# Low-part loads of a mixture-of-experts stage asked for one run of groups earlier, with two more tables for it

## What is computed

```python
x = x + xattn(layernorm(x), ctx)       # similarities to 1601 context rows, softmax, 2048 -> 512 projection
x = x + attention(layernorm(x))        # 16 heads, causal over 64 tokens
x = x + ffn(layernorm(x))              # below
# ffn: 8 experts, each token goes to its top 2, and a shared expert takes all
logits = x @ w_router.T
expert_weight, expert_idx = top_k(softmax(logits), 2)
inter = square(relu(tokens_of_expert @ w1[e].T))       # 512 -> 512
out_e = inter @ w2[e].T                                # 512 -> 512, times the gate, added to its token
shared = square(relu(x @ ws1.T)) @ ws2.T               # 512 -> 1024 -> 512
```

## Time and profile before

| | |
|---|---|
| median of the runs | 1274.67 us |
| the profiled execution | 1274.44 us, span 1272.7 us |
| TensorE (PE) busy | 1244.0 us, 98% |
| VectorE (DVE) busy | 755.4 us, 59% |
| ScalarE (ACT) busy | 376.5 us, 30% |
| groups of the experts | from 1034 us to 1262 us |
| end | last indirect DMA issued at 1266.45 us |

### The profile page before, as it was taken

One profiled execution on the slowest core, in us unless ns is written; L12 is line 12 of the kernel. 1 busy time (PEld: TensorE's weight loads), 2 busy tenths in 40 slices (PEclk: granted clock), 3 DMA queues, 4 the chain that ended last, 5 costly groups with the idle time before them and its releaser, 6 DMA issues.

```text
span 1272.7 us, 22853 instructions
## 1 busy us (share of the span) xinstructions
PE 1244.0 (98%) x7814; PEld 862.4 (68%) x7815; DVE 755.4 (59%) x1421; ACT 376.5 (30%) x613; POOL 205.1 (16%) x176
## 2 busy tenths in 40 slices
PE   6999999999999999999999999999999999999997
PEld 3444444444444444467888888899989888888886
DVE  3556555655544444478988877857546355555554
ACT  2322211212121111144554554442323233333322
POOL 1000000000000000004222223340531012222222
PEclk9999999999999999999999999999999999999999
DMA  9999999999999999843787788750643678777774
GB/s 357 417 421 419 418 419 422 422 422 421 408 410 389 397 392 393 330 149 107 291 269 261 271 289 313 258 127 1 232 166 132 204 222 186 185 158 158 178 157 92
DMA packets 105433, 358.39 MB, mean 282 GB/s; under 512 B 19872, under 2 KB 40352, under 8 KB 90784
## 3 DMA queue, kind: packets, MB, share of 16 engines
q1 hardware_dynamic: 96880, 337.97, 71.1%
q0 software_dynamic: 8496, 19.73, 7.7%
HBM read 352.80 MB, written 67.78 MB: 330 GB/s over the span
## 4 chain that ended last, share of the span: by engine, by line
PE 83%; DMA 9%; DVE 3%; issue 2%; SPq 1%; ACT 1%; POOL 0%; ACTq 0%; DVEq 0%; POOLq 0%
PE ps L2001 14%; PE ps L1889 13%; PE ps L2073 11%; PE ps L2063 10%; DMA parts_low<-split 5%; PE ps L2363 5%; PE ps L2355 5%; PE ps L2358 5%; PE ps L1964 4%; PE ps L1847 3%; PE ps L1979 2%; DMA high<-parts_low 1%; PE ps L1939 1%; DMA arena<-moe_in 1%; PE ps L1946 1%
## 5 line engine op out<-in xcount | busy, mean ns | idle before, releaser
L2073 PE MATMUL ps<-split 128*128 128x256 f32 x1536 | 194.2, 285 | 3.1 <-DVE split L1336 2.7
L2001 PE MATMUL ps<-arena 128*64 128x512 f32 (+1 forms) x832 | 192.6, 595 | 0.0
L2073 PEld LDWEIGHTS ps<-split 128*128 128x128 f32 x1536 | 187.1, 191 | 8.0 <-issue 6.5
L1889 PE MATMUL ps<-arena 128*64 128x512 f32 (+1 forms) x1024 | 178.7, 505 | 3.9 <-DMA arena<-ctx_t 2.1
L1889 PEld LDWEIGHTS ps<-arena 128*64 128x64 f32 x1024 | 66.0, 138 | 124.2 <-issue 119.4
L2001 PEld LDWEIGHTS ps<-arena 128*64 128x64 f32 (+1 forms) x832 | 58.4, 137 | 112.8 <-issue 112.1
L1232 DVE SCALAR_TENSOR_TENSOR arena<-arena,hbar 128x512 f32<-128x512 f32 x128 | 90.5, 749 | 67.8 <-PE ps L1964 66.1
L768 ACT ACTIVATE arena<-ps 128x512 f32<-128x512 f32 (+1 forms) x93 | 52.3, 581 | 240.5 <-PE ps L1964 180.2
L758 POOL DMA_INDIRECT out<-arena,token_i x39 | 60.5, 1552 | 246.2 <-DVE arena L1803 130.5
L651 POOL TENSOR_TENSOR arena<-arena,row_b 128x512 f32 (+1 forms) x16 | 20.3, 1273 | 476.0 <-DVE arena L1106 448.2
L2063 PE MATMUL ps<-split 128*128 128x512 f32 x384 | 96.9, 401 | 0.1
(11 more groups left out here) (249 smaller groups left out, 1947.3 us busy)
## 6 DMA issues: line engine op xcount, KB each, us to landing
arena<-ctx_t SPq DMA_DIRECT2D x122, 800.5 KB, 14.1
high<-parts_low SPq DMA_DIRECT2D x78, 1024.0 KB
arena<-ctx_n SPq DMA_DIRECT2D x96, 768.0 KB, 10.7
arena<-ctx_n SPq DMA_DIRECT2D x32, 1024.0 KB, 11.6
parts_high<-split SPq DMA_DIRECT2D x16, 1024.0 KB, 8.7
parts_low<-split SPq DMA_DIRECT2D x16, 1024.0 KB, 10.6
moe_in<-zero SPq DMA_DIRECT2D x3, 3328.0 KB, 18.3
stage_raw<-w1t SPq DMA_DIRECT2D x8, 1024.0 KB, 6.5
```

The source lines that it names most:

```text
L1889: last = mm(bank(n)[S * h:S * (h + 1), 0:w], qT[:, k, S * h:S * (h + 1)], ctxT[h][:, k, at_j:at_j + w], start=(k == 0), stop=(k == KD - 1))
L2001: last = mm(bank(7)[S * h:S * (h + 1), :], ET[0:w, c, S * h:S * (h + 1)], ctxN[h][0:w, c, :], start=(c == 0), stop=(c == JC - 1))
L2073: last = mm(dst[:, 2 * P * m:2 * P * (m + 1)], w[a][:, k, c], tokens[b][:, k, :], start=(k + i == 0), stop=(k == KD - 1 and i == 2))
```

## The change

The low parts of the next run are now asked for when a run begins, so that a whole run of groups lies between request and use. For that there are two more tables. `needed_loads`, on DVE behind pair 5 of the shared expert, makes `need_i`: a group's expert with its odd flag, and on top of it the semaphore count at which its low parts are there. TensorE reads this table in place of `eg_i` and waits for that count in a register; it no longer waits for the requests of groups in between. `next_runs`, behind pair 6, makes `next_i`: for each group the expert of the next run, with a flag on the first group of a run, which is where the request moves data. SP reads `next_i` for every request of `w1` and again for every one of `w2`. Both tables lie in memory that is free by then (`causal`, `lg`). There are as many requests and as many moved megabytes as before.

In SP's loop `load_slots(g + 3)` now comes first. Then comes the request for `w1` of group `g + 1`, which brings the next run's part where `g + 1` begins a run, and that for `w2` of group `g`. In iteration 0 the request of group 0 for `w1` stands ahead, behind the slots of group 3. The load of `w2`'s high part of expert 3 goes from before the rows of group 0 to behind them, since the DVE tiles beside which it lies are in use until `next_runs` is done.

```diff
--- before.py
+++ after.py
@@ -107,6 +107,8 @@
 
         slot_i = [sb(f"slot_i{k}", [P, T], I32) for k in range(2)]
         eg_i = sb("eg_i", [P, GT], I32)
+        next_i = lg[:, :, :].rearrange("p t e -> p (t e)")[:, 0:GT].bitcast(I32)
+        need_i = causal[:, 0:GT].bitcast(I32)
         token_i = sb("token_i", [P, GT], I32)
         landed_i = [sb(f"landed_i{i}", [P, GT], I32) for i in range(NY)]
         idx = [[sb(f"idx{k}{i}", [P, 1], I32) for i in range(4)] for k in range(2)]
@@ -544,32 +546,27 @@
             sp.wait_ge(x3_ready, TH)
             store_rows(slice(TH // 2, TH))
 
-            group = {}
-
-            def read_group(g):
-                group[g] = sp.value_load(eg_i[0:1, g:g + 1], min_val=0, max_val=2 * E - 1)
-                group.pop(g - 3, None)
-
-            def load_low(g, parts, places, back):
-
-                odd, e = group[g] >= E, group[g] & (E - 1)
-                if g > 0:
-                    sp.wait_ge(back, 16 * g)
+            def load_low(value, parts, places, back, at, cond):
+
+                odd, e = (value & (2 * E - 1)) >= E, value & (E - 1)
+                if at > 0:
+                    sp.wait_ge(back, 16 * at)
                 sp.dma_start(all_high[:, bass.ds(places[0] + odd * (places[1] - places[0]), KD * D)].bitcast(F32),
-                             parts[bass.ds(e * P, P), :], cond=group[g] != group[g - 1] if g > 0 else None
-                             ).then_inc(back, 16)
-
-            def load_low1(g):
-                load_low(g, parts_low[0], LOW1, low1_back)
-
-            def load_low2(g):
-                load_low(g, parts_low[1], LOW2, low2_back)
-
-            read_group(0)
+                             parts[bass.ds(e * P, P), :], cond=cond).then_inc(back, 16)
+
+            def first_low(parts, places, back):
+                value = sp.value_load(eg_i[0:1, 0:1], min_val=0, max_val=2 * E - 1)
+                load_low(value, parts, places, back, 0, None)
+
+            def next_low(g, parts, places, back):
+                value = sp.value_load(next_i[0:1, g:g + 1], min_val=0, max_val=4 * E - 1)
+                load_low(value, parts, places, back, g + 1, value >= 2 * E)
+
+            first = parts_low[0], LOW1, low1_back
+            second = parts_low[1], LOW2, low2_back
+
             sp.wait_ge(x3_out, 32)
             load_w2(ARENA + KD * D, 7, 8)
-            sp.wait_ge(token_ready, NY)
-            load_w2(3 * KD * D, 3, 4)
             sp.wait_ge(lg_done, T)
             sp.wait_ge(h2lo_ready, T)
             load_w1(1, 2)
@@ -577,7 +574,7 @@
             store_rows(slice(TH, TR))
             for i in range(NH):
                 sp.wait_ge(scat[i], 32 * (T // NH))
-            load_low1(0)
+            first_low(*first)
 
             def load_slots(g):
 
@@ -590,6 +587,8 @@
 
             load_slots(0)
             sp.dma_start(of_slot[:, :, :], info_v).then_inc(info_in, 16)
+            sp.wait_ge(token_ready, 2 + NY)
+            load_w2(3 * KD * D, 3, 4)
             sp.wait_ge(sh_done, 4 * (TA // 2))
             load_w1(0, 1)
             load_w2(0 * KD * D, 0, 2)
@@ -599,26 +598,27 @@
             load_w2(4 * KD * D, 4, 6)
             sp.wait_ge(shlo_ready, 4 * (TA // 2))
             load_slots(2)
-            read_group(1)
             sp.wait_ge(shlo_used, 1)
-            load_low2(0)
+            first_low(*second)
             sp.wait_ge(shared_done, TA)
-            load_low1(1)
             sp.wait_ge(x3_ready, T)
             store_rows(slice(TR, T))
 
             for g in range(GT):
-                if g + 2 < GT:
-                    read_group(g + 2)
-                    sp.wait_ge(in_done, g + 1)
-                    load_low1(g + 2)
                 if g + 3 < GT:
                     sp.wait_ge(xgT_ready, g + 2)
                     load_slots(g + 3)
+                if g == 0:
+                    next_low(0, *first)
+                if g + 2 < GT:
+                    sp.wait_ge(in_done, g + 1)
+                    next_low(g + 1, *first)
                 if g + 1 < GT:
                     if g > 0:
                         sp.wait_ge(y_done, g)
-                    load_low2(g + 1)
+                    next_low(g, *second)
+            sp.wait_ge(low1_back, 16 * GT)
+            sp.wait_ge(low2_back, 16 * GT)
             sp.wait_ge(x3_out, 16 * 4)
 
 
@@ -747,7 +747,7 @@
                             moe_in, bass.IndirectOffsetOnAxis(ap=idx[k][i][:, :], axis=0), hs_rows[i], None
                         ).then_inc(scat[i], 16)
 
-            pool.wait_ge(token_ready, 1 + NY)
+            pool.wait_ge(token_ready, 3 + NY)
             pool.wait_ge(x3_out, 16 * 4)
             for g in range(GT):
                 landed = [pool.value_load(landed_i[i][0:1, g:g + 1], min_val=16, max_val=16 * (GT // NY + 2))
@@ -1745,6 +1745,35 @@
                     step(v.tensor_reduce(landed, passed, AX, ALU.add))
                     v.tensor_scalar(landed_i[i][:, :], landed, 16.0, 16.0, ALU.mult, ALU.add).then_inc(token_ready, 1)
 
+            def needed_loads():
+
+                step(v.tensor_scalar(run, run, NY - 1.0, None, ALU.add))
+                step(v.tensor_tensor(gcmp, run.unsqueeze(2).to_broadcast([P, GT, E]),
+                                     ends.unsqueeze(1).to_broadcast([P, GT, E]), ALU.is_gt))
+                step(v.tensor_tensor(gcmp, gcmp, ends.unsqueeze(1).to_broadcast([P, GT, E]), ALU.mult))
+                step(v.tensor_reduce(rank, gcmp, AX, ALU.max))
+                step(v.tensor_scalar(landed, run, 0.0, None, ALU.is_gt))
+                step(v.tensor_tensor(rank, rank, landed, ALU.add))
+                step(v.scalar_tensor_tensor(eg_f, rank, 2.0 * E, eg_f, ALU.mult, ALU.add))
+                v.tensor_scalar(need_i, eg_f, 2.0 * E, None, ALU.add).then_inc(token_ready, 1)
+
+            def next_runs():
+
+                step(v.tensor_tensor(gcmp, ends.unsqueeze(1).to_broadcast([P, GT, E]),
+                                     iota_g.unsqueeze(2).to_broadcast([P, GT, E]), ALU.is_le))
+                step(v.scalar_tensor_tensor(gcmp, gcmp, 4.0 * GT, ends.unsqueeze(1).to_broadcast([P, GT, E]),
+                                            ALU.mult, ALU.add))
+                step(v.tensor_reduce(rank, gcmp, AX, ALU.min))
+                step(v.tensor_tensor(gcmp, ends.unsqueeze(1).to_broadcast([P, GT, E]),
+                                     rank.unsqueeze(2).to_broadcast([P, GT, E]), ALU.is_le))
+                step(v.tensor_reduce(eg_f, gcmp, AX, ALU.add))
+                step(v.tensor_scalar(eg_f, eg_f, float(E - 1), None, ALU.min))
+                step(v.scalar_tensor_tensor(eg_f, turn, -float(E), eg_f, ALU.mult, ALU.add))
+                step(v.tensor_tensor(landed, run, iota_g, ALU.is_equal))
+                step(v.tensor_scalar(rank, rank, float(GT), None, ALU.is_lt))
+                step(v.tensor_tensor(landed, landed, rank, ALU.mult))
+                step(v.scalar_tensor_tensor(eg_f, landed, 2.0 * E, eg_f, ALU.mult, ALU.add))
+                v.tensor_scalar(next_i, eg_f, float(E), None, ALU.add).then_inc(token_ready, 1)
 
             def scattered_norm(turn, half):
                 for b in range(2 * half, 2 * half + 2):
@@ -1767,8 +1796,10 @@
                 shared(p, scatter=p - 1)
             shared(4, scatter=3)
             run_starts()
-            for p in range(5, TA // 2 - 1):
-                shared(p)
+            shared(5)
+            needed_loads()
+            shared(6)
+            next_runs()
             last_pair = TA // 2 - 1
             square(last_pair, 0)
             square(last_pair, 1)
@@ -2376,14 +2407,14 @@
                 if last and now:
                     inter_T(g)
                 if now:
-                    e, odd = expert(g)
+                    e, odd, need = expert(g)
                     three_passes(
                         bank(2), xT_p, lambda k: w1_high[:, bass.ds(e, 1), k, :].rearrange("p o f -> p (o f)"),
                         at_place(LOW1, odd),
                         (lambda: pe.wait_ge(xhi_ready, g + 1), lambda: pe.wait_ge(xlo_ready, g + 1),
-                         lambda: pe.wait_ge(low1_back, 16 * g + 16))).then_inc(in_done, 1)
+                         lambda: pe.wait_ge(low1_back, need))).then_inc(in_done, 1)
                 if last:
-                    e_last, odd_last = expert(g - 1)
+                    e_last, odd_last, need_last = expert(g - 1)
                     if second:
                         pe.wait_ge(w2_in, 16 * 6)
                     elif now:
@@ -2393,15 +2424,16 @@
                         bank(3 if now else 4), iT_p if now else xT_p,
                         lambda k: all_high[:, bass.ds(at_e + k * D, D)], at_place(LOW2, odd_last),
                         (lambda: pe.wait_ge(iT_ready, g), lambda: pe.wait_ge(ilo_ready, g),
-                         lambda: pe.wait_ge(low2_back, 16 * g)),
+                         lambda: pe.wait_ge(low2_back, need_last)),
```

(5 more changed lines are left out.)

## The result

| | before | after |
|---|---|---|
| median (lowest to highest), 21 runs each | 1274.67 us (1272.39 to 1279.62) | 1280.06 us (1277.58 to 1283.72) |
| ratio after to before, 95% interval | | 1.0041, 1.0032 to 1.0050 |
| profiled execution, span | 1274.44, 1272.7 us | 1280.06, 1278.3 us |

The change costs 5.4 us where 10.6 were forecast (from the median; the sum itself was 10.9 on the profiled execution). The sign, the first stop and its reason are those of the forecast, and the time is in its range. What was too large is above all one term, the other run changes: 6.3 us were forecast, and 0.3 came. The forecast stops of 1 to 2 us at groups 13, 17, 21, 30 and 34 did not come: group 13 lost 0.22 us, the other four nothing.

A forecast was written before the change was run, and what follows sets the result against it. TensorE was taken as the bound, one group behind another at 5.92 us, with SP's queue nearly full. 6.0 + 6.3 + 1.0 - 2.4 = 10.9 us on 1274.44 gave 1285.3 us; range 1276.5 to 1292.5.

The forecast's parts named there:

- The sign: Whole kernel: the change makes it slower, chance 0.75.
- the first stop: Ahead of group 4: its rows come 7.0 us late behind two 1 MB waits, and TensorE stops for 6.0 us.
- the other run changes: Later run changes: SP's cycle of 25.1 us against TensorE's 23.7 costs about 1.3 per gap of four, 6.3 us.
- Clock: Behind the stop at group 4: TensorE's clock may fall to half, costing 1.0 us, at most 1.7.
- Removed stops: Groups from 1034 us on: TensorE's waits for low parts, with restarts and slower pace behind them, go: -2.4 us.
- Costed at 0: New DVE tables, the moved w2 load, and TensorE's masking instruction and register wait per product: 0 us.
- Rival 1: Stop at group 4 alone, no later loss: 1277.5 us, up to 1279; chance 0.22.
- Rival 2: At group 4, copies of rows overtake the 1 MB load: 1274.0 us, not slower; chance 0.10.
- rivals 3 to 5: Everything at the upper end, 1293.7 us, 0.12; high parts late, 1288, 0.06; low parts still last, about 1287, 0.02.
- rival 3: Everything at the upper end: first stop 7.5, each gap of four 2.5, clock 1.7; 1293.7 us, chance 0.12.

The follow-up runs named there:

- e5: The kernel before without GpSimd's scatter-adds of the experts' results and the waits on them (output incomplete): 1265.16 us, one run.
- e6: The changed kernel without GpSimd's scatter-adds of the experts' results and the waits on them (output incomplete): 1271.13 us, one run.
- e4: The changed kernel with 20 matmuls into an unused bank between groups 3 and 4 in TensorE's queue: 1279.13 us, ratio to before 1.0053.
- e1: The changed kernel with the second run's request for w2 moved one iteration later, behind the copies of group 4's rows: 1281.26 us, one run.
- e3: The changed kernel with the old requests' place and rule, keeping new tables, register waits and moved w2 load: 1274.86 us, ratio to before 1.0003.
- e9: The changed kernel with row copies one group earlier from group 4 on, and one SP table read per group: 1272.86 us, ratio to before 0.9989.

## Why the prediction was right in kind and wrong in size

- **First stop, forecast 6.0: 4.92 us.** The walk through SP's queue held. The copies of group 3 took 3.21 us for 2.36, `w1` landed in 4.98 for 6.8, and group 4's rows 7.74 us behind `w2`'s request for 8.6, so they landed at 1054.86 and not 1056.4. The slack of 1.0 us was right. The lower bound stood at 4.5; its own landing times, 6.2 and 8.2, give 5.0, so 4.92 lies just under it.
- **The other run changes, forecast 6.3: 0.33 us. This is the term that failed.** From the request for `w1` to the landing of the rows behind `w2` the forecast had 6.8 + 1.9 + 9.15 = 17.85 us. Measured at the seven later changes: 16.2, 18.4, 15.2, 15.4, 17.5, 15.0, 15.1, mean 16.1. Most of the difference is the last piece: the rows landed 7.6 to 8.0 us behind `w2`'s request, not 9.15, and `w1` in 6.4 on average, not 6.8.

  With the other 7.25 us of the sum, taken as forecast, SP's cycle is 23.4 us, just under TensorE's 23.7. The trace bears that out: from one such landing of rows to the next the five gaps of four took 26.5, 23.3, 23.6, 22.9 and 23.8 us. The first of them, with the slowest `w1` (8.5 us), used up the 2.2 us that were in hand at group 9 and stopped TensorE for 0.22. The two of the seven that are long, 18.4 and 17.5, are the two in front of the late rows at groups 13 and 26.

  Why shorter: the landing times came from the earlier trace rows, where each load had been issued into GpSimd's adds; the change asks for `w2` at another moment, with few adds under way (25 to 40 of their packets in the window at six of the seven changes, 187 at the other), and its landing fell to 5.4 to 5.7 us there and 6.7 at the other. A duration was carried over as if it belonged to the load, while it belonged to the load and to what ran beside it. e5 and e6 show that directly.

  The working had a slip besides: 25.1 less 23.7 is 1.4 and not 1.3, and five times that is 7.0 and not 6.3. That nothing is left in hand after the first stop was wrong as well: rows landed 3.6 to 6.2 us early at groups 5 to 8, since SP went on while TensorE ran slow and through a run of five.
- **Clock, forecast 1.0: 2.0 us** (e4). The slow stretch lasted 6.83 us, not 3.4 as in the earlier trace rows, and 4.3 us of it lay behind the stop. The Trainium skill, "TensorE: Matmul & The Clock Gate", part 1, says that an idle TensorE is put back to half its clock and must earn the full one by work. The traces agree: the fall came at each of the three long stops (after, e1, e6), and the whole 1.7 kept by that rule was nearer to 2.0.
- **Removed stops, forecast -2.4: -1.56 us.** The stops went. The slower pace from group 27 on, 0.7 us of the 2.4, did not: it is there in every trace, e5 and e6 included, so it was no part of the prize.
- **Costed at 0:** tables, moved load, register waits cost nothing (e3). One thing was missed, slow reads of TensorE's table, 0.21 us.
- Sum: 4.92 + 2.00 + 0.54 - 1.56 = 5.90, less 0.34 ahead of the groups. That the stop and the clock together come to 6.92 us where 7.0 were forecast is luck: one was 1.1 too large and the other 1.0 too small. Rival 1, the stop at group 4 alone, was nearest in mechanism; 1277.5 to 1279 was its time, since it had 0.5 for the clock. Rival 2 is out, since the copies never overtook the load. Of rivals 3 to 5 nothing came as they said but the clock's 1.7 in rival 3.

## What to carry to other kernels

A request that waits in an in-order queue is priced by what stands behind it: walk the queue in its new order, and put what the next stage needs first ahead of the first wait. A transfer's landing time is not its own: before it is carried over, look at which queues shared the DMA engines in its window, and whether they will in the new one. Where a sum rests on a cycle that is within a few per cent of what covers it (25.1 against 23.7), the term can be nothing or many times the difference, and neither the forecast nor its chances should lean on one of the two.

## What the runs showed of the hardware

- 1 MB from DRAM landed 4.8 to 5.5 us after its issue without the adds (e5, e6), 5.0 to 5.7 with at most 76 of their packets in its window, and 7.3 to 8.6 with 200 to 280 (before, after).
- TensorE's clock was at 0.50 for 6.83 us in the changed kernel and in e1, beginning 2.0 and 3.3 us after the engine fell idle and ending 4.3 and 6.0 us after it began again, though the stops are of like length (4.5 and 4.2 us in TensorE's rows). The cost was 2.0 and 2.8 us. In e6 the stretch of 6.83 us began 0.5 us before TensorE did and cost 3.0. A stretch of 3.41 us early in the kernel cost 1.63 us in the five traces that have it.
- A register load of TensorE from SBUF takes 0.30 us, but now and then 0.7 to 1.2. Of 17 over 0.7 us in six traces 14 began 3.0 to 3.7 us after SP issued a 1 MB load, and none was seen without the adds (152 reads). But three traces with the adds (before, e3, e9) had none either, with 30 reads at that same distance behind a load, so the cause stays open.
- The pace of a group is 5.927 us up to group 26 and 5.987 from 27 on, in nearly every trace and with nothing late. The second product of each group, its last 12 matmuls, takes that bit longer (2.73 us, then 2.78). It isn't the adds (e5, e6), and not the requests (e3); its cause is open.
